# Perceiver kernel on one core: VectorE work of the passage from the experts to the second cross-attention, cut in pieces and set between the evictions

## The reference, cut to what matters

```python
x = x + _L0_ffn_ref(_layernorm(x), gate_w, gate_bias, Wg, Wu, Wd, Sg, Su, Sd)      # experts
x = x + _L1_xattn_ref(_layernorm(x), ctx_1024, mask, Wq, bq, Wkv, bkv, Wo, bo)     # 16 heads of 32
...
def _L1_xattn_ref(q, kv, key_padding_mask, Wq, bq, Wkv, bkv, Wo, bo):
    Q = (q @ Wq + bq)                       # queries need the finished x
    K, V = split(kv @ Wkv + bkv)            # keys and values need the context alone
    attn = softmax(where(mask, -inf, Q @ K.T * scale))
    return (attn @ V) @ Wo + bo
```

## Time and profile before

| | |
|---|---|
| Time of the runs, median (lowest to highest) | 1735.79 us (1731.43 to 1737.17) |
| The profiled execution's own time | 1739.35 us |
| Its span, first to last instruction | 1737.6 us |
| PE busy | 1665.8 us, 96% of the span |
| DVE, ACT, POOL busy | 957.6, 626.4, 461.7 us |
| Mean granted TensorE clock | 0.986 |
| The passage in this execution | first key group at 697.08 us, first turn of unit 0 at 772.23 us |

### The profile page before, as it was taken

One profiled execution on the slowest core, in us unless ns is written; L12 is line 12 of the kernel. 1 busy time (PEld: TensorE's weight loads), 2 busy tenths in 40 slices (PEclk: granted clock), 3 DMA queues, 4 the chain that ended last, 5 costly groups with the idle time before them and its releaser, 6 DMA issues.

```text
span 1737.6 us, 34823 instructions
## 1 busy us (share of the span) xinstructions
PE 1665.8 (96%) x13779; PEld 1360.2 (78%) x13781; DVE 957.6 (55%) x2061; ACT 626.4 (36%) x844; POOL 461.7 (27%) x454
## 2 busy tenths in 40 slices
PE   8999999999999999699999999999999999999796
PEld 5665687777777777568898988889888898888583
DVE  4878576666666665444444444454454444544476
ACT  1232255555555555112424224242242332423122
POOL 3100445555555555210303003021030210300110
PEclk9999999999999999799999999999999999999898
DMA  8012499999999999300202002020020200202200
GB/s 293 13 38 95 172 322 335 332 333 338 344 343 343 341 341 299 96 1 2 77 6 77 6 1 77 6 77 6 2 77 6 77 6 2 77 2 71 83 2 25
DMA packets 68474, 223.25 MB, mean 128 GB/s; under 512 B 9010, under 2 KB 26674, under 8 KB 58496
## 3 DMA queue, kind: packets, MB, share of 16 engines
q1 hardware_dynamic: 54016, 196.29, 32.3%
q0 software_dynamic: 14336, 25.19, 6.8%
HBM read 208.07 MB, written 21.76 MB: 132 GB/s over the span
## 4 chain that ended last, share of the span: by engine, by line
PE 86%; DMA 5%; DVE 3%; ACT 3%; issue 2%; POOL 1%; SPq 0%; POOLq 0%; DVEq 0%; ACTq 0%
PE PS L1306 18%; PE PS L1297 16%; PE PS L2033 10%; PE PS L2056 8%; PE PS L1341 6%; PE PS L1324 5%; PE PS L1358 3%; PE PS L398 3%; DMA S<-moe_rows,gcol 2%; PE PS L754 2%; PE PS L456 2%; DMA R<-in_w_gu 2%; PE PS L419 1%; PE PS L770 1%; PE PS L2017 1%
## 5 line engine op out<-in xcount | busy, mean ns | idle before, releaser
L1306 PE MATMUL PS<-S_r 128*128 128x256 f32 x2496 | 330.4, 287 | 6.2 <-DVE kh0l L1494 6.2
L1306 PEld LDWEIGHTS PS<-S_r 128*128 128x128 f32 x2496 | 306.2, 190 | 33.5 <-issue 24.6
L1297 PE MATMUL PS<-S_r 128*128 128x384 f32 (+1 forms) x1536 | 308.1, 350 | 0.0
L2033 PE MATMUL PS<-S_r,R_r 128*128 128x352 f32 x1152 | 299.0, 350 | 1.7 <-DVE R_r L2161 1.7
L1297 PEld LDWEIGHTS PS<-S_r 128*128 128x128 f32 x1536 | 266.8, 188 | 10.8 <-issue 3.0
L2033 PEld LDWEIGHTS PS<-S_r,R_r 128*128 128x128 f32 x1152 | 199.8, 189 | 20.5 <-issue 18.6
L1452 ACT COPY S<-PS 128x512 f32<-128x512 f32 (+1 forms) x128 | 64.4, 503 | 299.2 <-PE PS L1341 299.2
L1243 POOL COPY S<-qbd 128x128 f32<-128x128 f32 x32 | 9.4, 293 | 611.0 <-PE PS L1324 588.1
L1505 DVE CUSTOM_DVE_ANT_0 R<-PS,maskadd 128x384 f32<-128x384 f32 (+1 forms) x256 | 136.2, 570 | 29.0 <-PE PS L1324 26.9
L1487 DVE TENSOR_TENSOR R<-PS,vbias 128x256 f32<-128x256 f32 (+1 forms) x208 | 88.0, 423 | 103.7 <-PE PS L1306 100.5
L1896 DVE TENSOR_TENSOR R_r<-R,S_r 128x1408 fp32r<-128x1408 f32 x64 | 101.2, 1623 | 73.5 <-ACT S_r L1888 73.5
(11 more groups left out here) (260 smaller groups left out, 2484.5 us busy)
## 6 DMA issues: line engine op xcount, KB each, us to landing
R<-in_w_gu SPq DMA_DIRECT2D x34, 1408.0 KB, 12.1
R<-in_w_dna SPq DMA_DIRECT2D x50, 512.0 KB, 7.1
qbd<-in_w_gu SPq DMA_DIRECT2D x16, 1408.0 KB, 11.2
S<-in_w_gu SPq DMA_DIRECT2D x16, 1408.0 KB, 12.2
S<-in_ctxT SPq DMA_DIRECT2D x24, 768.0 KB, 4.7
R<-in_w_dnb SPq DMA_DIRECT2D x50, 192.0 KB, 9.2
xnT<-in_w_dna SPq DMA_DIRECT2D x16, 512.0 KB, 7.2
S<-in_ctxT SPq DMA_DIRECT2D x8, 898.0 KB, 5.1
```

The lines of the kernel that those rows point to most:

```text
L1297: last = nc.tensor.matmul(PS[:, bank, 0:n], w3[0][:, cc, f0:f0 + P], x3[i][:, cc, 0:n], start=(cc == 0 and w3 is wkv_hi and x3 is ctx_hi), ...
L1306: last = nc.tensor.matmul(PS[:, bank, 0:256], x3[need][:, cc, k0:k0 + P], w3[1][:, cc, f0:f0 + 256], start=(cc == 0 and w3 is wkv_hi and x ...
L2033: last = nc.tensor.matmul(PS[:, gu, 0:I], x3[:, c, :], w3[:, c, gu, :], start=(c == 0 and x3 is hi[0] and w3 is hi[1]), stop=(c == NC - 1 ...
```

## The change

It does five things:

1. POOL no longer makes the rest of chunk 1 of batch 0. DVE makes the rests of chunks 1, 2 and 3, each in two halves (`first_rest(c, h)`, two of the four feature blocks each).
2. DVE's rests, mask pieces, sums and moments are cut in pieces and stand between the evictions of `PRE[0]`.
3. The value groups `v9`, `v10` and `v11` move from `PRE[1]` to `PRE[0]`; `PRE[1]` becomes `s0 k2 s1 k3 v12 s2 s3`.
4. The queries go to PSUM banks 2 to 5 in place of 0 to 3, so `s0` (banks 0 and 1) no longer has to wait for their eviction.
5. POOL takes each query feature as soon as it is evicted, not after all four.

```diff
-        PRE = ["k0 v0 v1 v2 k1 v3 v4 v5 v6 v7 v8", "s0 k2 v9 s1 k3 v10 s2 v11 s3 v12"]
+        PRE = ["k0 v0 v1 v2 k1 v3 v4 v5 v6 v7 v8 v9 v10 v11", "s0 k2 s1 k3 v12 s2 s3"]
...
-            pool.wait_ge(q_ready, 3 * NC)
+            pool.wait_ge(q_ready, 2 * NC + 1)
             take_q(0, 0, 0)
+            pool.wait_ge(q_ready, 2 * NC + 2)
             take_q(0, 1, 0)
...
-            q_pe(pe, wq1, 3, 2, bank=0)
+            q_pe(pe, wq1, 3, 2, bank=2)
...
-            for c in (2, 3):
-                n = KC[c][1]
+            def first_rest(c, h):
+                n, half = KC[c][1], slice(NC // 2 * h, NC // 2 * h + NC // 2)
                 dve.wait_ge(hi_ready, c + 1)
-                nc.vector.tensor_tensor(ctx_lo[c][:, :, 0:n], ctx_raw[c][:, :, 0:n],
-                                        ctx_hi[c][:, :, 0:n].bitcast(F32), ALU.subtract).then_inc(lo0_ready, 1)
-            for c in range(4):
-                set_mask(0, c)
+                nc.vector.tensor_tensor(ctx_lo[c][:, half, 0:n], ctx_raw[c][:, half, 0:n],
+                                        ctx_hi[c][:, half, 0:n].bitcast(F32), ALU.subtract).then_inc(lo0_ready, 1)
...
+            first_rest(1, 0)
+            first_rest(1, 1)
             dve.wait_ge(ld_vb1, 16)
-            for w in PRE[0]:
-                token(-1, 3, w)
+            made(("k", 0), ("v", 0), ("v", 1))
+            first_rest(2, 0)
+            first_rest(2, 1)
+            made(("v", 2), ("k", 1))
+            first_rest(3, 0)
+            made(("v", 3))
+            first_rest(3, 1)
+            made(("v", 4))
+            set_mask(0, 0)
+            set_mask(0, 1)
+            made(("v", 5))
+            set_mask(0, 2)
+            set_mask(0, 3)
+            made(("v", 6))
             dve.wait_ge(acc_in, 32)
+            sums(0)
+            link(sums(1))
+            made(("v", 7))
+            sums(2)
+            link(sums(3))
+            made(("v", 8))
+            moments(0)
+            link(moments(1))
+            made(("v", 9))
+            moments(2)
+            link(moments(3))
+            made(("v", 10))
             for t in range(NT):
-                last = nc.vector.tensor_tensor(x[:, t, :], x[:, t, :], x_odd[:, t, :], ALU.add)
+                last = nc.vector.bn_aggr(mv[:, t, :], st[:, t, :])
             link(last)
-            ln_dve(dve, link, 3)
+            nc.vector.tensor_scalar(rstd[:, :], mv[:, :, 1], EPS, None, ALU.add).then_inc(mv_ready, 1)
+            dve.wait_ge(rstd_ready, MV[3] + 1)
+            scaled(0)
+            scaled(1)
+            made(("v", 11))
+            scaled(2)
+            scaled(3)
...
-                    if k in (1, 2):
-                        ctx_rest(0, k - 1)
+                    if k == 1:
+                        ctx_rest(0, 0)
```

More of the change, by code:

```diff
@@ L326, in out_bias @@
             nc.gpsimd.tensor_tensor(x[:, t, :], x[:, t, :], bias_r[:, :], ALU.add).then_inc(xb_ready, 1)
[L328 to L340, removed]
         def ln_pool(pool, n):
@@ L1180, in perceiver @@
         GROUPS = [(dc, w) for dc in range(4) for w in MADE[dc]]
-        assert len(GROUPS) % 2 == 0 and PRE_MADE[-2:] == MADE[3][-2:] and len(PRE_MADE) == len(MADE[3])
+        assert len(GROUPS) % 2 == 0 and len(PRE_MADE) == len(MADE[3])
         KTS = [[kt for kt in range(KT_N) if kt // 4 == tg] for tg in range(4)]
@@ L1258, in xattn_pool @@
             for dc in (2, 3):
+                pool.wait_ge(q_ready, 2 * NC + dc + 1)
                 pool.wait_ge(sx_made, 8 * (dc - 1))
@@ L1278, in group @@
                     if made is not PRE_MADE:
-                        pe.wait_ge(lo_ready, 2 + 4 * b + need + 1)
-                    elif need < 2:
-                        pe.wait_ge(lo_ready, need + 1)
+                        pe.wait_ge(lo_ready, 4 * b + need + 2)
+                    elif need:
+                        pe.wait_ge(lo0_ready, 2 * need)
                     else:
-                        pe.wait_ge(lo0_ready, need - 1)
+                        pe.wait_ge(lo_ready, 1)
                 if not (made is PRE_MADE and made.index(w) < 2):
-                    dc2, (kind2, i2) = (dc, made[made.index(w) - 2]) if made is PRE_MADE else GROUPS[at - 2]
-                    b2 = b if at >= 2 else b - 1
+                    if made is PRE_MADE:
+                        b2, dc2, (kind2, i2) = b, dc, made[made.index(w) - 2]
+                    elif b == 0 and at < 2:
+                        b2, dc2, (kind2, i2) = -1, 3, PRE_MADE[at - 2]
+                    else:
+                        b2, (dc2, (kind2, i2)) = b if at >= 2 else b - 1, GROUPS[at - 2]
                     if kind2 == "k":
@@ L1574, in xattn_dve, with made @@
-            for c in range(4):
-                set_mask(0, c)
-            dve.wait_ge(ld_vb1, 16)
-            for w in PRE[0]:
-                token(-1, 3, w)
-            dve.wait_ge(acc_in, 32)
+                nc.vector.tensor_tensor(ctx_lo[c][:, half, 0:n], ctx_raw[c][:, half, 0:n],
+                                        ctx_hi[c][:, half, 0:n].bitcast(F32), ALU.subtract).then_inc(lo0_ready, 1)
+            def made(*which):
+                for w in which:
+                    token(-1, 3, w)
@@ new lines, in sums, with moments, scaled @@
+            def sums(t):
+                return nc.vector.tensor_tensor(x[:, t, :], x[:, t, :], x_odd[:, t, :], ALU.add)
+            def moments(t):
+                return nc.vector.bn_stats(st[:, t, :], x[:, t, :])
+            def scaled(t):
+                nc.vector.tensor_scalar(xn[:, t, :], x[:, t, :], mv[:, t, 0:1], rstd[:, t:t + 1],
+                                        ALU.subtract, ALU.mult).then_inc(xn_ready, 1)
+            first_rest(1, 0)
+            first_rest(1, 1)
+            dve.wait_ge(ld_vb1, 16)
@@ L1584, in xattn_dve @@
+            dve.wait_ge(rstd_ready, MV[3] + 1)
[4 more added lines that the diff above has]
+            scaled(3)
             xt_copy(dve, nc.vector.tensor_copy, 3, (1, 3))
-            q_dve(dve, 2, 2, bank=0)
+            q_dve(dve, 2, 2, bank=2)
             for w in PRE[1]:
```

## The result

| | before | changed |
|---|---|---|
| median of 4 runs (lowest to highest), us | 1736.45 (1731.43 to 1737.17) | 1718.05 (1715.83 to 1718.75) |
| profiled execution: time, span, granted clock | 1739.35, 1737.6, 0.986 | 1717.77, 1716.0, 0.994 |
| PE busy | 1665.8 (96%) | 1659.1 (97%) |

The changed kernel takes 0.9897 of the time of before, with an interval of 0.9879 to 0.9915: 18.4 us less by the medians, where 13.95 were forecast (with a fourth run of before, its median is 1736.45 and no longer 1735.79). The time lies in the range, 3.75 us under the forecast.

A forecast was written before the change was run, and what follows sets the result against it. PE, busy 96% of the span, was taken as the bound, so time could come only from its idle and low-clock stretches. Terms summed to 13.95 us gained, from 1735.79 to 1721.8 us; range 1716.5 to 1727.5.

The forecast's parts named there:

- Wait of `v1`: PE idle ahead of `v1`: `k0` evicted sooner, the 6.21 us stretch shrinks to 1.35, 4.85 us gained.
- Clock of `v1` and `v2`: `v1` and `v2` took 5.30 us at clock 0.50; at full clock 2.3 us would be gained.
- DVE between the groups: `v3` to `v11`: DVE's 12.3 us of work nearly even with PE's 12.7; small waits, 0.5 us lost.
- Wait for the normalised x: PE idle ahead of the transposes: the 7.77 us stretch becomes 2.6, 5.2 us gained.
- Transposes: Transposes and their copies, 4.55 us before: 1.3 us gained at full clock, 0.9 at low clock; 0.9 counted.
- queries: Queries, 15.89 us before, 13.7 at full clock: 2.2 us gained or nothing, by the clock; nothing counted.
- the paragraph on the clock: From `v11`'s end to the queries: unpriced clock cost between nothing and about 3 us; a fall was assumed.
- The first rival: Clock holds from `v11` through transposes and queries: 16.55 us gained in all, 1719.2 us; chance 0.22.
- Wait of `s0`: PE idle ahead of `s0`, the first score piece: free banks and early query taking remove it, 3.2 us gained.
- Moved groups: `v9` to `v11` moved ahead of the queries: uncovered waits of 1.35 before `s3`, 0.85 later; 2.0 us lost.
- margin of under 2 us: Accumulator load lands about 713 us, DVE asks for it at about 714.5; no cost forecast.
- DVE's queue becomes the bound: Value groups wait on DVE's slower work or the accumulator, 2 to 3 us: 11 gained, 1724.8 us; chance 0.13.

The follow-up runs named there:

- second profile of before: Kernel before, run once more with no edit and profiled: 1733.98 us, ratio 0.9991 (0.9977 to 1.0004); its passage took 76.85 us.

## Why the prediction was right, and where it was not

The mechanism was the one forecast: the evictions were what PE waited for, and PE's idle stretches shrank where and nearly as far as the terms say. The passage gave 14.58 against 13.95. The terms, one by one:

1. *Wait of `v1`* (4.85): 4.32. DVE took `kh0l` up at 696.57, 0.51 after ACT's end at 696.06, where I had counted nothing, so 1.94 was left and not 1.35. Rests and masks ahead of `k0`'s eviction put 3.17 of it back.
2. *Clock of `v1` and `v2`* (2.3): **0.66, the step that failed**. I argued that a wait of 3.17 had left the clock at 1.00, "so one of 1.35 should too". It was one observation. A wait of 3.16 ahead of `s0` cost the clock in the second profile of before and did not with the queries back in banks 0 to 3, and 1.94 cost it in four profiles (the change in two, the queries in banks 0 to 3, the value groups back) and not in a fifth (the sums in one block). Against the second profile of before, in which this stretch took 4.72 us, the gain is only 0.25.
3. *DVE between the groups* (-0.5): overstated. 13.26 us for nine groups looks like the 12.7 + 0.5 forecast, but 12.7 was too little: six groups took 8.85 before, and three more at 1.42 make 13.11. With the sums in one block, so without them between `v7` and `v11`, the nine took 13.10. So 0.15 was lost. DVE was not yet the bound, though from `v7` on its evictions came 1.65 apart; its head start of two banks was about used up at `v11`.
4. *Wait for the normalised x* (5.2): 5.60; 2.17 was left and not 2.6. The blocked sums gave the 7.76 back.
5. *Transposes* (0.9) and 6. *queries* (0): 1.31 and 1.99. **Here the paragraph on the clock failed the other way**: it took the cost of a fall ("I take the cost"), and the clock held. The first rival, worth 1.3 and 2.2, was true of this stretch. My argument by the length of the stretch without other matmuls does not decide it: the same 5.4 us of it stayed at 1.00 in five profiles (the change and the earlier `k0` with `v12` moved, two each, and the queries in banks 0 to 3) and fell in four (rests and masks first, chunk 1's rest on POOL, the earlier `k0` alone and with halved loads). In the first two of the four it was back by the queries, which took 13.97 us; in the other two they took 15.75 and 15.83.
7. *Wait of `s0`* (3.2): 3.16; shown twice, by undoing the banks and POOL's early taking (3.17 longer) and by putting these two alone into the kernel before. The term names both ("banks are now free and its query was taken long before"); the trace lays it to the second.
8. *Moved groups* (4.25 out and back, 2.0 lost in waits): 4.41 out, with the 0.15 of term 3 in it; 1.98 gained from `s0` on against 2.25; waits of 1.34 and 0.80 where 1.35 and 0.85 stood.

So the clock was called wrongly in both places, 1.6 too much in the first and 2.4 too little in the second, and the errors nearly cancel. The sum is right to 0.6 in part by luck.

The accumulator landed at 709.0 and DVE wanted it at 710.30: the "margin of under 2 us" was 1.3, from about 1.5 forecast, and this too is two errors that cancel. The step "SP loads `x_odd` 3.7 after a scatter's issue ends" failed: it was 5.85, so the accumulator landed 17.8 us behind `k0` and not 15.9. And DVE came to it 19.06 behind `k0` and not 17.4, in the main by the low clock of `v1` and `v2`. At full clock there (1.52 us less) it would have come at about 17.5, with no margin left; this is an estimate from the rows above. The four runs in which DVE comes 16.0 to 17.2 us behind `k0` and the loads are whole all wait for the accumulator. The rival "DVE's queue becomes the bound" did not occur in the change, but its second half, the wait for the accumulator, is the next bound of the kernel, and behind it DVE's pace of 1.65 us. "Hidden" and "slower" are excluded by the result; the clock was not low again in the changed kernel behind `v2`.

The medians differ by 18.4 and the passage by 14.6 (15.5 against the second profile of before). The 3 to 4 us between them are not explained by the passage of one profile. The start of the passage may hold some of it: three profiles with the old order ahead of it start at 697.08, 691.95 and 695.01 (mean 694.7), eleven with the new one between 688.6 and 694.9 (mean 691.4). Whether the expert stage gains some 3 us from the change (POOL has one subtraction less beside the scatters) or only its executions differ is open; the version with chunk 1's rest on POOL starts at 691.31, which speaks for the second, as far as one profile can.

## What to carry to other kernels

Where one engine's queue feeds the bottleneck, put its long work behind the eviction that the bottleneck waits for, in pieces that together with one eviction are about as long as the bottleneck's own groups; here nine groups of 1.42 us took up 8.8 us of rests, masks, sums and moments and lost 0.15, though piece and eviction were 1.65 at the end. Price the clock apart from the idle time, as a term with two values, and take more than one profile before saying which value a short wait has. When a wait is removed, look for the load that had been in time only thanks to it: here the accumulator, with 1.3 us to spare, took 1.6 us of the next improvement. And before laying such a wait to a late load, compare both times with a fixed mark: with chunk 1's rest on POOL the load came 0.2 us later and the engine that wanted it 1.9 us earlier.
